# Attention's q and k blocks: one half issued by SyncE and one by ScalarE, each a block earlier, from one point of the program

## What is computed

```python
def _L0_gnn_ref(x, edge_index, edge_attr, ...):
    summed = segment_sum(edge_attr, col)          # 106250 edges of 64 values into 6250 nodes
    agg = summed / maximum(count, 1.0)[:, None]
    h = relu(concatenate([x, agg]) @ W1 + b1)
    return x + h @ W2 + b2

def _L0_mix_ref(x, ...):                          # 8 heads of 64
    q, k, v = split(x @ W_qkv.T + b_qkv); q = sigmoid(q); k = sigmoid(k)
    ...                                           # i, i_hat and o_hat: sums over all tokens
    vw = v * softmax(o_hat, axis=1)
    kv = einsum("bshd,bshe->bsde", k, vw)
    r = einsum("bshd,bsde->bshe", q / i, kv) * sigmoid(i_hat)
    return r.reshape(B, S, E) @ W_out.T + b_out
```

## Time and profile before

| | us |
|---|---|
| median of 3 executions | 2092.01 (2088.13 to 2098.23) |
| the profiled execution, own time | 2093.92 |
| its span | 2092.2 |
| PE busy | 1857.4 (89%) |
| POOL busy | 1323.1 (63%) |
| DVE busy | 1221.7 (58%) |
| ACT busy | 636.3 (30%) |

### The profile page before, as it was taken

The page is one execution under the profiler, slowest core; times in us unless marked ns, Lnnn a source line. Parts: engine busy times, 40 slices in busy tenths (PEclk is TensorE's granted clock), DMA queues, the critical chain, the costliest instruction groups (busy, mean ns, idle before and its releaser), DMA issues. The chain is left out here.

```text
span 2092.2 us, 31150 instructions
## 1 busy us (share of the span) xinstructions
PE 1857.4 (89%) x10776; PEld 1497.0 (72%) x10776; DVE 1221.7 (58%) x3872; ACT 636.3 (30%) x1522; POOL 1323.1 (63%) x850
## 2 busy tenths in 40 slices
PE   2799999999999999788874898898958999997798
PEld 1688888888888888644433676777746888886686
DVE  3644453444434343177854676766758888884675
ACT  1423332223322232111112444434333434343210
POOL 4888888888888888768887877777888100000000
PEclk9999999999999999876586899998989999999899
DMA  8977888777777777799799999999979777653884
GB/s 291 229 147 149 148 160 156 151 144 153 148 163 149 139 142 129 156 256 199 141 301 213 212 198 220 218 224 198 229 157 221 235 224 222 210 172 112 302 287 153
DMA packets 501056, 400.77 MB, mean 192 GB/s; under 512 B 355604, under 2 KB 368148, under 8 KB 500900
## 3 DMA queue, kind: packets, MB, share of 16 engines
q1 hardware_dynamic: 378836, 369.73, 61.0%
q0 software_dynamic: 119952, 28.99, 21.7%
q10 hardware_dynamic: 2112, 0.07, 0.1%
HBM read 244.05 MB, written 154.62 MB: 191 GB/s over the span
## 5 line engine op out<-in xcount | busy, mean ns | idle before, releaser
L297 POOL DMA_INDIRECT table<-edge_ring,edge_row x831 | 1312.2, 1579 | 311.4 <-issue 228.1
L237 DVE SCALAR_TENSOR_TENSOR edge_sel<-edge_dst_all,edge_dst_f,upper 128x128 f32<-128x128 int16 x831 | 318.0, 439 | 93.1 <-PE edge_sum L249 75.0
L365 PE MATMUL pr_out_bank<-pr_norm_xT_hi,pr_w_hi 128*128 128x512 f32 (+1 forms) x832 | 327.6, 394 | 0.0
L365 PE MATMUL pr_out_bank<-pr_norm_xT_lo,pr_w_hi 128*128 128x512 f32 (+1 forms) x832 | 319.3, 384 | 0.0
L365 PE MATMUL pr_out_bank<-pr_norm_xT_hi,pr_w_lo 128*128 128x512 f32 (+1 forms) x832 | 318.6, 383 | 0.0
L249 PEld LDWEIGHTS edge_sum<-edge_attr,edge_sel 128*128 128x128 f32 x1662 | 230.5, 208 | 79.3 <-DVE edge_sel L237 49.7
L249 PE MATMUL edge_sum<-edge_attr,edge_sel 128*128 128x65 f32 x1662 | 236.9, 291 | 42.1 <-DVE edge_sel L237 40.8
L2343 POOL DMA_INDIRECT ex_w_raw<-in_w_exp,ex_row x4 | 5.1, 1266 | 304.2 <-issue 304.2
L365 PEld LDWEIGHTS pr_out_bank<-pr_norm_xT_lo,pr_w_hi 128*128 128x128 f32 x832 | 156.6, 188 | 32.2
L262 ACT ACTIVATE edge_ring<-edge_sum 128x260 f32<-128x260 f32 (+1 forms) x209 | 80.1, 384 | 326.6 <-PE edge_sum L249 255.8
L365 PEld LDWEIGHTS pr_out_bank<-pr_norm_xT_hi,pr_w_lo 128*128 128x128 f32 x832 | 157.0, 189 | 28.4
(11 more groups left out here) (208 smaller groups left out, 3278.2 us busy)
## 6 DMA issues: line engine op xcount, KB each, us to landing
edge_dst_all<-dst SPq DMA_DIRECT2D x103, 256.0 KB
edge_attr<-in_edge_attr SPq DMA_DIRECT2D x103, 256.0 KB
qk_halves<-pr_stage SPq DMA_DIRECT2D x48, 512.0 KB
h_pre_T<-pr_stage SPq DMA_DIRECT2D x48, 512.0 KB
gn_pre<-h_pre_T SPq DMA_DIRECT2D x48, 512.0 KB, 7.0
done<-qk_halves SPq DMA_DIRECT2D x16, 1024.0 KB
table<-edge_ring,edge_row POOLq DMA_INDIRECT x831
pr_norm_x<-in_x SPq DMA_DIRECT2D x12, 1024.0 KB
```

The costliest lines, as they stand in the source:

```text
L237: op = dve.scalar_tensor_tensor(out=self.sel[q][0:rows, j, 0:rows], in0=self.dst_all[k][0:rows, t:t + m * (rows - 1) + 1:m], scalar=self.d ...
L297: pool.indirect_dma_start(self.c.table[t], bass.IndirectOffsetOnAxis(ap=self.row[k][0:rows, j:j + 1], axis=0), self.sums[k][0:rows, j, :], ...
L365: mm = pe.matmul(out, a, c, start=first and i == 0, stop=last and i == n - 1)
```

## The change

q and k are still loaded once per block into the same tiles, 24 transfers of 512 KB each and a tail. Three things differ. The load for block b + 2 is issued in block b, where it was issued in block b + 1. Half 0 is issued by SP behind x of b + 1, half 1 by ACT between `spread_mix(b + 1, 3)` and the third `keep`. Both wait for `mixed` of b * 4 + 3, that is for mixing step 2 of block b, which PE begins after the block's last scores. The wait of SP for `scored` is gone.

```diff
--- before.py
+++ after.py
@@ -1403,6 +1403,20 @@
 
         return (b - 1) * (CH + 1) + 3
 
+    def load_half(eng, b, half):
+
+        for side, dst in enumerate((q[b % 2], kk[b % 2])):
+            eng.dma_start(dst[half * HDIM:(half + 1) * HDIM, :, :].rearrange("d (x o) t -> d x (o t)", x=2),
+                          c.qk[side, 2 * b + half, :, :, :].rearrange("(x d) o t -> d x (o t)", x=2)
+                          ).then_inc(qk_in[b % 2], 16)
+
+    def load_tail(eng):
+
+        for side, dst in enumerate((q[FULL % 2], kk[FULL % 2])):
+            for x in range(2):
+                eng.dma_start(dst[0:HDIM, x * CH:(x + 1) * CH, 0:TAIL],
+                              c.qk[side, 2 * FULL, x * HDIM:(x + 1) * HDIM, :, 0:TAIL]).then_inc(qk_in[FULL % 2], 16)
+
     EARLY_FREE = 11
     FIRST = 4
 
@@ -1412,19 +1426,6 @@
         return spread(share.quads(b)[FIRST if b == 0 else 0:], 6)
 
     def sp_program(sp):
-        def load_qk(b):
-            for half, r in enumerate([BT // 2, BT // 2] if b < FULL else [TAIL]):
-                for side, dst in enumerate((q[b % 2], kk[b % 2])):
-                    rows = slice(half * HDIM, (half + 1) * HDIM)
-                    if r == HALF:
-                        sp.dma_start(dst[rows, :, :].rearrange("d (x o) t -> d x (o t)", x=2),
-                                     c.qk[side, 2 * b + half, :, :, :].rearrange("(x d) o t -> d x (o t)", x=2)
-                                     ).then_inc(qk_in[b % 2], 16)
-                    else:
-                        for x in range(2):
-                            sp.dma_start(dst[rows, x * CH:(x + 1) * CH, 0:r],
-                                         c.qk[side, 2 * b, x * HDIM:(x + 1) * HDIM, :, 0:r]).then_inc(qk_in[b % 2], 16)
-
         def load_v(b):
             rows = c.v.rearrange("t (h e) -> (t h) e", h=HEADS)
             full = sizes[b] // GT
@@ -1444,7 +1445,8 @@
                 sp.dma_start(x[b % 2][0:n, 0, :], c.x[block_at(b), :]).then_inc(x_in[b % 2], 16)
 
         sp.wait_ge(before.io_mm, EARLY_FREE)
-        load_qk(0)
+        load_half(sp, 0, 0)
+        load_half(sp, 0, 1)
         weights.load(sp)
         load_v(0)
         sp.dma_start(bias[:, :], c.b2.partition_broadcast(P)).then_inc(bias_in, 16)
@@ -1459,7 +1461,8 @@
             if i == 0:
                 load_first_mix(sp, 0)
         before.over(sp)
-        load_qk(1)
+        load_half(sp, 1, 0)
+        load_half(sp, 1, 1)
         load_x(0)
         weights.wait(sp)
 
@@ -1478,8 +1481,6 @@
                 edges.load_ahead(sp, *batch)
             if b + 1 < NB:
                 if b:
-                    sp.wait_ge(scored, b * STEPS)
-                    load_qk(b + 1)
                     sp.wait_ge(mixed, b * STEPS)
                 load_v(b + 1)
                 for ahead in [1, 2] if b == 0 else [b + 2]:
@@ -1493,6 +1494,12 @@
                 if b:
                     sp.wait_ge(rest_ready, b * CH)
                 load_x(b + 1)
+            if b + 2 < NB:
+                sp.wait_ge(mixed, b * STEPS + 3)
+                if b + 2 < FULL:
+                    load_half(sp, b + 2, 0)
+                else:
+                    load_tail(sp)
             for batch in batches[2:]:
                 edges.load_ahead(sp, *batch)
         me.preload(sp)
@@ -1644,6 +1651,9 @@
                 spread_mix(b + 1, 2)
                 by_token(b + 1, 0)
                 spread_mix(b + 1, 3)
+                if b + 2 < FULL:
+                    act.wait_ge(mixed, b * STEPS + 3)
+                    load_half(act, b + 2, 1)
                 keep(quads, 3)
                 if b + 1 < FULL:
                     by_token(b + 1, 1)
```

## The result

The changed kernel takes 2104.14 us (median of 13 runs, 2089.39 to 2118.84), the kernel before, run beside it, 2094.43 us (2087.64 to 2103.31). The ratio is 1.0046, with a 95% interval of 1.0029 to 1.0064: slower by some 10 us, where 18 us less were forecast. The profiled execution took 2104.1 us, with a span of 2102.4 against 2092.2.

A forecast was written before the change was run, and what follows sets the result against it. PE's wait for `at_kt` bounds attend's loop: 21.2 us of wait plus 12 of clock give 33, cut to 17.6 by POOL's ring. 2093.9 - 17.6 = 2076.3, as a median 2074 us; range 2061 to 2087.

The forecast's parts named there:

- Wait removed: Attend's loop: k lands in time, so PE's 25.7 us wait for `at_kt` shrinks by 21.2 us.
- What else moves: SP's order and the factors: SP's queue: a new wait for mixing step 2 costs nothing, and the 12.21 us stand on the factors' issue becomes shorter.
- the prediction's own last sign of being wrong: Anywhere in the kernel: a PE wait over 2 us per block standing at another place would show the forecast wrong.
- Clock that comes back: PE in attend's loop: 24 of 39.3 us at half clock return to full clock, saving 12 us.
- POOL's ring as the cap: End of attend: batch 104's ring place frees only at 1519.0 us, leaving 17.6 of the 33 us saved.
- ACT's two issues at nothing: ACT, each block: two added issues take under 1.7 us together, within 7.2 us of slack, so cost nothing.
- Rival 4: ACT stands on a full queue ahead of its result copies, 55 us lost against 33 gained: 2114 us; chance 0.06.
- Halves against each other: DMA transfers of q and k: two halves at once might help or merely serialize; the sum needs neither.
- rival 1: Attend's loop: DMA engines are the bound, the wait only moves; 8 to 14 us saved, 2078 to 2084; chance 0.27 including nothing.
- Attend's end carries to the program's end: Gnn stage after attend: its start and PE chain move along with attend's end, some 18 us earlier.
- P: Theory from the experiments, SP's queue: factors' small packets are drawn out on meeting ACT's large ones, delaying x behind them.
- Q: Rival theory from the experiments: ACT's 1 MB goes ahead of SP's store and x, whatever the packets.

The follow-up runs named there:

- act_both: Changed kernel with both halves of q and k issued in ACT's queue, only the tail by SP; 2074.15 us, ratio 0.9925.
- wide_after: Changed kernel with whole blocks' factors loaded as 128 packets of 1 KB, not 4096 of 32 bytes; 2071.41 us, ratio 0.9903.
- wide_before: Kernel before the change with whole blocks' factors loaded as 128 packets of 1 KB, not 4096 of 32 bytes; 2075.69 us, ratio 0.9930.
- act_both_wide: act_both with whole blocks' factors loaded as 128 packets of 1 KB, not 4096 of 32 bytes; 2089.51 us, ratio 0.9983.
- act_both_meet: act_both with SP's factor load moved to the common point of ACT's four transfers; 2077.51 us, ratio 0.9930.

## Why the prediction was wrong

- *Wait removed.* Right for PE: its 25.7 us for `at_kt` are gone. Not for the load: ACT's wait for k was to be under 3 us and is 24.9, hidden behind that for x. The load was to have about 25 us. In the block shown SP's part of it was issued at 1310.54, behind the late x, 16.0 us ahead of the copy at 1326.53, which still had to wait for it.
- *What else moves: SP's order and the factors.* **This is the step that failed.** It said of SP's queue that "some microseconds there cost nothing", put no term for it into the sum, and expected the stand on the factors' issue to become shorter. That stand did (12.21 us to 5.98), but the one behind it, on the store, grew from 3.0 us to 8.6 in the median. Cover was named for v and edges. For x, issued behind the factors and the store and due soon, none was looked for. DVE waited for it 49.6 us in all, up to 13.5 at once, and PE 32.7 us behind DVE. This is the prediction's own last sign of being wrong, a wait of PE over 2 us per block at another place.
- *Clock that comes back.* Wrong with it: 74 us of the loop at half clock for 39, where 24 of the 39 were to go. The prediction's rule, half the time at half clock, would make the 35 us more cost 17; PE is busy only 5.6 us longer, so most of them lie in its waits.
- *POOL's ring as the cap.* Right in the place and near in the size, where the loop was quick enough to reach it: in the seven kernels from 2069 to 2078 us the sixth tile of batch 96 started between 1517.3 and 1529.9 us, for the 1517.5 taken, and the forecast for this cap was 2074. In the changed kernel it never bound; POOL's first of its last 58 tiles starts there at

```profile
1521.18 1.66 POOL L297 DMA_INDIRECT table<-edge_ring,edge_row  x1 [0.30 <-issue]
```

- *ACT's two issues at nothing.* Right: 0.58 to 1.6 us each, no stand. Rival 4 is out.
- *Halves against each other, and rival 1.* Rival 1 came nearest. It named waits left on x, and half of its sign is there, a DMA share above 1.12 (it is 1.13); the other half, PE's waits on `at_kt` or `at_v`, is not, and it had a gain of 8 to 14 us. Its reason, full engines, is refuted by act_both and wide_after. The share counts time in which packets of 32 bytes hold an engine: from 1295 to 1298 us in the kernel before, SP's packets held 87.4% of the engines for 0.22 MB. No rival had the trigger: a second queue's large packets beside the first queue's small ones. SP's 12.21 us on the factors' issue was read rightly as a stand on a full queue: it is as long in wide_before. The sign of the small packets was the stand behind it, 3.0 us on the store, where the issue of x, as large, takes 0.85 us; the question what happens when such packets have to share was not asked.
- *Attend's end carries to the program's end.* Right: the first product of attend's tail is 10.6 us later (1552.38 for 1541.76), and the end 10.2 us.

Open is the share of P and of Q in the loss, and why POOL's own waits grew in act_both_wide and wide_after. A deeper ring, the next bound, was not tried, nor a layout in memory that would give the factors wide packets and keep the reference's result.

## What to carry to other kernels

Before a load is put on a second queue, list what the first queue holds at that moment and what is due soonest behind it. A transfer of many small packets there was the danger in this kernel, however few its bytes: coalesce it, or place the new load later (0.87% here by moving two issues). And if a queue is split, try giving the second one the whole of the far-ahead load; here that left the first queue shorter for its near-due transfers, and was worth 1.2% against the split by halves.

## What the runs showed of the hardware

- Packets of 32 bytes that pass in 3 us beside POOL's queue alone (1295 to 1298 us, before) took from 1298 to 1307 in the changed kernel, after four us in which hardly one passed. ACT's queue had 58.6% of the engines from 1298 to 1300, 13.6% from 1300 to 1303 and 2.3% after, so the last four us are not time taken by ACT's packets. Elsewhere the two queues did share: in act_both from 1241 to 1250 us ACT's had 435 packets (81.5% of the engines' time) and SP's 615 (18.0%). The Trainium skill (DMA: Bandwidth & Descriptors, Queues, rings and completion order) states that each engine takes turns between queues packet by packet. The second stretch agrees in kind, for by turns a queue of small packets gets few bytes; the first, 37 packets against 150 in 1294 to 1298, does not follow from turns alone, unless SP's packets were not there yet to take theirs, which no run shows.
- Engines can be nearly idle inside a full queue. From 1303 to 1307 us, while SP stood on its issue:

```profile
DMA  6312410311211212121222121181111009979885
...
DMA packets 809, 0.11 MB, mean 27 GB/s; under 512 B 802, under 2 KB 802, under 8 KB 808
```

It does not take ACT's queue. The kernel before has one us of it, from 1294 to 1295, just ahead of the factors' packets (busy tenths of 0 to 3). In act_both_meet it comes at the end of the factors' packets, when ACT's queue has none. From 1310 to 1311 us:

```profile
DMA  1100010001000111245534223111059999999001
```

```profile
q1 hardware_dynamic: 248, 0.01, 13.1%
```

That the last packets lie on a few engines, for which the issue of the next transfer has to wait, is my reading; no run separates it.
- The 4096 packets of 32 bytes cost 0.7% of this kernel even without ACT's queue beside them (wide_before), for 128 KB a block.
